# Attention kernel with a head mix: 64x64 mixing, the turn of E by R in two row halves, and k one step earlier

## The chip, the cores and the metric

One NeuronCore of a Trainium2 chip runs the whole program. The metric is the device time of one execution in microseconds (us). The engines are TensorE (PE: matrix products; its weight loads are shown as PEld), VectorE (DVE), ScalarE (ACT), GpSimd (POOL) and SyncE (SP, which issues most DMAs). Everything is fp32. An fp32 product shows in the trace as two passes, each a weight load and a MATMUL: "x8" for four products is eight passes.

## The reference

The input x has 8 batches of 512 tokens with 256 features. The program is half a step of an FFN block, an attention block and half a step of the FFN block again; only the attention is touched (and its constants, which are built during the first FFN). Cut to what matters:

```
q, k, v = x@Wq, x@Wk, x@Wv             # 16 heads of 64; 4 memory keys/values are put in front
dots = (l2norm(q) . l2norm(k)) * 10     # [16 heads, 512 queries, up to 516 keys]
dots = einsum('hg,bgij->bhij', W_pre_th, dots)    # every head becomes a mix of the 16 heads
dots = mask(causal); keep the 64 largest of a row, the others are masked
attn = softmax(dots)
attn = einsum('hg,bgij->bhij', W_post_th, attn)   # mixed over the heads again
out  = (attn @ v) * head_scale * sigmoid(x@Wg + bg) @ Wo
```

## The kernel before

**Units of work.** A tile t is 128 tokens (32 tiles; t % 4 is its place in its batch, here called tile 0 to 3 of the batch). A half u is 64 tokens. A group n is 8 queries with all 16 heads, 128 rows in all; a tile has 16 groups, and its step g (0, 2, ... 14) handles the pair of groups g and g+1. The width of a group is its number of live keys: 12 for the first of a batch, 8 more for each next one, 516 for the last. So tile 0 has widths 12 to 132, tile 1 140 to 260, tile 2 268 to 388, tile 3 396 to 516.

**The way of a group.** (1) PE computes raw scores of a half in four quarters (`score`, L1025): 64x64 products, four of them next to each other in the array, into bankD; ACT copies them to SC (L1241). (2) SP brings a group's scores with one DMA into 128 rows, raw[n] (L951). (3) PE mixes the heads (`mix`, L1036): one 128x128 stationary matrix `mixpre`, which is zero between different queries, and raw[n] streaming, into bankB; ACT writes it to S (L1252, L1255). (4) POOL adds the diagonal mask (L1387) and sets a first threshold (L1396), DVE takes row maxima and finds the 64th largest (`row_max`, `select_pair`), ACT counts signs (L1262, L1270) and takes the exponential (L1278), DVE zeroes what is below the limit and sums (L1559), then takes the reciprocal (L1563). (5) POOL scales the second mixing matrix by it: R = mixpost * rinv, 128x128 (L1403). (6) PE turns and mixes at once (`turn`, L1052): for each block of 128 keys E's block (128x128) is stationary and R (128x128) streams, which gives keys x (head, query) in bankC; a group of tile 0 has one block, of tile 3 four. ACT copies it into PT (`out_PT`, L1288). (7) PE multiplies PT with V (`attend`, L1078), and later projects (L1098).

**The order.** All engines run one loop over pairs n0, each with its own list of what comes in a step. PE in step n0 does mix(n0), a piece of projection, transpose or score, mix(n0+1), then turn(n0-6) and turn(n0-5), then another piece, then a piece of attend. The pieces: step 0 has xT (the transpose of the next tile's input) and the q projection of the next tile; step 2 score 0 and 1 of the second half (with the v projection in tile 1); step 4 score 2 (with v in tile 0) and the k projection of the next tile; step 6 score 3 and the gates; step 8 the transposes qT and kT (L1007); steps 10 to 14 the scores of the next tile's first half. ACT's list runs parallel to it: evict(n0), the first piece, evict(n0+1), sign counts, out_PT of the two groups turned, the second piece, exp of the pair before. `project_qk` on ACT (L1184, L1187) squares and copies q or k, and waits before k's square for `ssq_done` of q, since both use the tile qksq.

DVE sums the squares (`squares`, L1474, L1475): of q of tile t+1 at its own step 14 of tile t-1, of k at its step 2 of tile t; both in its list behind select_pair of that step. DVE is about two steps behind PE and ACT: select_pair of step 14 runs while PE is in steps 0 and 2 of the next tile. POOL makes the norms (`norm`, L1377 and L1381) at its steps 4 and 6; qT and kT on PE wait for them. The banks of bankD are used in one fixed order, the list `uses`; each use waits until ACT has read the banks' last one.

## Time and profile before

| | |
|---|---|
| median of 3 runs | 2355.67 us (2355.18 to 2355.76) |
| the profiled execution | 2356.68 us, its span 2354.8 us, mean granted clock of TensorE 0.952 of full speed |
| busy share of the span | PE 89%, PEld 58%, DVE 77%, ACT 68%, POOL 35% |
| L1052, turn: PE busy | 351.7 us for 2560 passes |
| L1036, mix: PE busy | 353.9 us for 1024 passes |
| L1025, scores: PE busy | 191.0 us for 2304 passes |

The attention takes the middle of the span, from about 207 to 2140 us; the two FFN blocks stand before and after it. Its eight batches repeat one pattern, slice by slice. Busy times of PE are modelled from the starts of pipelined instructions, so a duration of one MATMUL is longer than the step from one to the next; the starts are what tells the rate.

### The profile page before, as it was taken

What the parts mean: (1) busy time and instruction counts of PE and PEld (TensorE: products, weight loads), DVE (VectorE), ACT (ScalarE), POOL (GpSimd) and SP (SyncE); (2) the same over time, 40 slices, a digit from 0 to 9 for tenths busy, and PEclk for the clock granted to TensorE, in tenths of its full rate; (3) what the DMA queues carried; (4) which work ended last, traced back from release to release, by engine and by line L of the source; (5) the groups of instructions that cost most, each with busy time, mean ns of one, the idle gap of its engine ahead of it and who ended that gap; (6) DMA issues with size and microseconds to landing.
All of it is one profiled execution on the core that took longest, in us unless ns stands there. A gap on an engine that the chain in (4) does not pass through costs nothing. (4 is left out here: it accounts for less than half of the span.)

```text
span 2354.8 us, 55179 instructions
## 1 busy us (share of the span) xinstructions
PE 2106.7 (89%) x16059; PEld 1369.2 (58%) x16060; DVE 1803.1 (77%) x7282; ACT 1608.3 (68%) x4676; POOL 822.6 (35%) x2274
## 2 busy tenths in 40 slices
PE   7995699999999999999999999999899889985997
PEld 3433456666666666666666666666666666663433
DVE  6565389968996899689958995899589959993446
ACT  4442578857885788688858885888688758861543
POOL 3001444444444443444344434443443344311000
PEclk9996799999999999999999999999999999987998
DMA  5002012111211121012101211121012101212002
GB/s 175 0 0 85 22 40 61 43 25 43 61 43 26 43 61 43 25 43 61 43 25 43 61 43 25 43 61 43 26 43 61 43 23 41 58 38 87 1 0 72
DMA packets 113217, 104.69 MB, mean 44 GB/s; under 512 B 34449, under 2 KB 110865, under 8 KB 112913
## 3 DMA queue, kind: packets, MB, share of 16 engines
q1 hardware_dynamic: 108000, 96.65, 16.1%
q10 hardware_dynamic: 4912, 4.46, 0.6%
q8 instruction: 134, 2.20, 0.4%
q14 instruction: 171, 1.39, 0.2%
HBM read 19.14 MB, written 12.71 MB: 14 GB/s over the span
## 5 line engine op out<-in xcount | busy, mean ns | idle before, releaser
L1052 PE MATMUL bankC<-R,E 128*128 128x128 f32 x2560 | 351.7, 287 | 40.0 <-POOL R L1403 39.9
L1052 PEld LDWEIGHTS bankC<-R,E 128*128 128x128 f32 x2560 | 338.5, 202 | 76.3 <-POOL R L1403 43.9
L1036 PE MATMUL bankB<-raw,mixpre 128*128 128x76 f32 (+37 forms) x1024 | 353.9, 433 | 19.7 <-DMA raw<-SC 19.4
L1252 ACT ACTIVATE S<-bankB,aim_first 128x68 f32<-128x68 f32 (+56 forms) x456 | 232.3, 513 | 163.7 <-PE bankB L1036 163.3
L1499 DVE TENSOR_SCALAR_CACHE_REDUCE S<-S,minus_thr 128x68 f32<-128x68 f32 (+56 forms) x456 | 218.5, 515 | 139.4 <-POOL minus_thr L1396 137.8
L1387 POOL TENSOR_TENSOR S<-S,diagmask 128x8 f32<-128x8 f32 x512 | 106.8, 213 | 522.5 <-ACT S L1252 484.5
L1403 POOL TENSOR_SCALAR R<-mixpost,rinv 128x128 f32<-128x128 f32 x512 | 184.3, 372 | 284.9 <-DVE rinv L1563 284.5
L1559 DVE SCALAR_TENSOR_TENSOR E<-S,limit,E 128x68 f32<-128x68 f32 (+56 forms) x456 | 221.3, 521 | 35.1 <-ACT E L1278 5.2
L1278 ACT ACTIVATE E<-S,nmax 128x12 f32<-128x12 f32 (+56 forms) x512 | 240.0, 528 | 0.7 <-POOL nmax L1417 0.7
L1078 PEld LDWEIGHTS bankM<-PT,V 128*64 128x64 f32 x5120 | 179.0, 138 | 101.4 <-issue 90.9
L1036 PEld LDWEIGHTS bankB<-raw,mixpre 128*128 128x128 f32 x1024 | 159.7, 192 | 120.4 <-issue 82.5
L1078 PE MATMUL bankM<-PT,V 128*64 128x64 f32 x5120 | 227.8, 230 | 0.9 <-DVE gate L1483 0.9
L1025 PE MATMUL bankD<-KT,QT 64*64 64x132 f32 (+8 forms) x2304 | 191.0, 406 | 33.1 <-ACT SC L1241 23.6
L1288 ACT COPY PT<-bankC 128x512 f32<-128x512 f32 (+3 forms) x512 | 194.2, 432 | 36.4 <-PE bankC L1052 31.4
L1270 ACT ACTIVATE junk_side<-S 128x68 bf16<-128x68 f32 (+56 forms) x456 | 200.0, 448 | 15.8 <-DVE S L1499 15.8
L1377 POOL TENSOR_TENSOR rn<-ssq,neghalf 128x16 f32<-128x16 f32 x64 | 186.5, 2914 | 39.3 <-DVE ssq L1475 39.1
L1534 DVE MATCH_REPLACE8 near<-top,near 128x68 f32<-128x68 f32 (+56 forms) x456 | 200.1, 446 | 0.0
L1262 ACT ACTIVATE junk_first<-S 128x60 bf16<-128x60 f32 (+56 forms) x456 | 197.8, 447 | 0.3
L1529 DVE MAX8 top<-near 128x8 f32<-128x68 f32 (+56 forms) x456 | 187.7, 452 | 0.3
L1538 DVE MAX8 top<-near 128x8 f32<-128x68 f32 (+56 forms) x456 | 186.9, 450 | 0.3
L1241 ACT COPY SC<-bankD 128x136 f32<-128x136 f32 (+7 forms) x256 | 167.2, 653 | 21.6 <-PE bankD L1025 20.8
L1524 DVE TENSOR_SCALAR near<-S,flip 128x68 int32<-128x68 int32 (+56 forms) x456 | 150.1, 370 | 0.0
(177 smaller groups left out, 3935.4 us busy)
## 6 DMA issues: line engine op xcount, KB each, us to landing
X_first<-in_L_attn_x_dram ACTq DMA_DIRECT2D x8, 512.0 KB, 10.4
x<-X_first SPq DMA_DIRECT2D x8, 512.0 KB, 2.9
xt<-x SPq DMA_DIRECT2D x32, 128.0 KB, 2.4
x<-xt SPq DMA_DIRECT2D x32, 128.0 KB, 2.5
X_last<-x SPq DMA_DIRECT2D x8, 512.0 KB, 6.6
out_dram<-X_last SPq DMA_DIRECT2D x8, 512.0 KB, 2.8
raw<-SC SPq DMA_DIRECT2D x8, 258.0 KB, 2.9
raw<-SC SPq DMA_DIRECT2D x8, 254.0 KB, 3.1
```

The costliest lines, as they stand in the source:

```text
L1025: last = nc.tensor.matmul(bankD[cols, r, i * s[3]:(i + 1) * s[3]], QT[rows, pair, HALF * hh:HALF * hh + HALF], KT[rows, pair, first:first ...
L1036: last = nc.tensor.matmul(bankB[n % 2][:, 0:wide(n)], W.mixpre[:, :], raw[n % RAWS][:, 0:wide(n)], start=True, stop=True)
L1052: last = nc.tensor.matmul(bankC[n % 2][:, jb * P:(jb + 1) * P], E[n % EBUFS][:, jb * P:(jb + 1) * P], R[n % RBUFS][:, :], start=True, stop ...
L1078: last = nc.tensor.matmul(bankM[64 * lo:64 * lo + 64, pair * HALF:(pair + 1) * HALF], V[:, slot(t - blocks + 1 + jb), h * DH:(h + 1) * DH] ...
L1252: nc.scalar.activation(S[n % SBUFS][:, 0:wide(n)], src, ACT.Identity, bias=W.aim_first[:, group(n)]).then_inc(S_out, 1)
L1262: nc.scalar.activation(junk_first[n % 2][:, 0:w], S[n % SBUFS][:, 0:w], ACT.Sign, scale=-1.0, accum_out=below[:, col(n)]).then_inc(below_d ...
L1270: nc.scalar.activation(junk_side[n % 2][:, 0:w], S[n % SBUFS][:, 0:w], ACT.Sign, accum_out=signs[:, col(n)]).then_inc(signs_done, 1)
L1278: nc.scalar.activation(E[n % EBUFS][:, 0:w], S[n % SBUFS][:, 0:w], ACT.Exp, bias=nmax[:, col(n)]) \
L1288: last = nc.scalar.copy(PT[u % 2][:, 0:blocks, :, at:at + IG], bankC[n % 2][:, 0:blocks * P].rearrange("p (j h i) -> p j h i", h=H, i=IG))
L1499: nc.vector.tensor_scalar(row, row, minus_thr[:, col(n)], None, ALU.add, ALU.max, accum_out=rmax[:, col(n)]).then_inc(max_done, 1)
L1534: at[n] = step(nc.vector.match_replace(out=row, in_to_replace=top[n % 2][:, 8 * r - 8:8 * r], in_values=row, imm_value=-FMAX))
L1559: at[n] = step(nc.vector.scalar_tensor_tensor(out=E[n % EBUFS][:, 0:w], in0=S[n % SBUFS][:, 0:w], scalar=least, in1=E[n % EBUFS][:, 0:w], ...
```

## The change

It has four parts, and small ones that follow from them.

1. **Head mix in 64x64.** The queries of a pair of groups are dealt out so that the first 64 rows of raw hold four queries and the last 64 four others; mixpre becomes 64 columns wide. `mix_pair` computes both groups with four 64x64 products, one in each quadrant of the array (rows r, columns cols), into the two banks bankB, and comes at the start of a step; ACT evicts both groups right behind it. It takes the place of mix(n0) and mix(n0+1). The raw DMA of the even group brings 8 more columns.
2. **Scores in 64x32.** To put queries in that order, a score product is cut in two with 32 stationary columns each: 16 products of 64x64 for a half become 32 of 64x32, eight places in the array for each quarter. The copy to QT is cut in two (L1219).
3. **The turn in two row halves.** R becomes 128x64. `turn_pair` has for each group and block two products, one for each half of the rows: stationary 64x128 of E, streaming 64x64 of R, each half into its own bank of bankC; one increment for the pair. ACT's out_PT copies bank by bank, both groups in one instruction, with the same number of elements. The last group of a tile, whose memory-tail product needs all columns, gets a full matrix Rlast from POOL.
4. **k sooner.** The k projection moves from step 4 to step 2 on PE and ACT, score 1 from step 2 to 4, score 2 behind the turn of step 4, v of tile 1 from step 2 to 4; POOL's norms move from steps 4 and 6 to 2 and 4, and k's squares on DVE from step 2 to 0.

The core of the diff (the building of constants, which grows by 22 small DVE instructions, and the lists on ACT, which mirror PE's, are cut):

```diff
@@ -1018,46 +1031,58 @@
                     def emit():
                         first, quarters = (512, range(4)) if s[2] == "last" else (0, (q,))
                         for i, quarter in enumerate(quarters):
-                            for side_ in range(2):
+                            for c, side_ in ((0, 0), (0, 1), (1, 0), (1, 1)):
                                 for r in range(2):
-                                    rows, cols = slice(64 * r, 64 * r + 64), slice(64 * side_, 64 * side_ + 64)
-                                    pair = 4 * side_ + quarter
-                                    last = nc.tensor.matmul(bankD[cols, r, i * s[3]:(i + 1) * s[3]],
-                                                            QT[rows, pair, HALF * hh:HALF * hh + HALF],
-                                                            KT[rows, pair, first:first + s[3]],
+                                    rows, at = slice(64 * r, 64 * r + 64), 64 * c + 32 * side_
+                                    pair, lo = 4 * side_ + quarter, HALF * hh + 32 * c
+                                    last = nc.tensor.matmul(bankD[at:at + 32, r, i * s[3]:(i + 1) * s[3]],
+                                                            QT[rows, pair, lo:lo + 32], KT[rows, pair, first:first + s[3]],
                                                             start=True, stop=True, skip_group_check=True)
                         return last
                     pe_use(pe, s, emit)
 
-            def mix(n):
-                pe.wait_ge(raw_in[n % RAWS], 16 * (n // RAWS + 1))
-                if n >= 2:
-                    pe.wait_ge(S_out, n - 1)
-                last = nc.tensor.matmul(bankB[n % 2][:, 0:wide(n)], W.mixpre[:, :], raw[n % RAWS][:, 0:wide(n)],
-                                        start=True, stop=True)
-                if is_wide(n):
-                    if n // GPT >= 2:
-                        pe.wait_ge(x_added, n // GPT - 1)
-                    last = nc.tensor.matmul(bankT[:, P:P + MEM], W.mixpre[:, :], raw[n % RAWS][:, 512:J],
-                                            start=True, stop=True)
-                last.then_inc(mixed, 1)
-
-            def turn(n):
-                t, g = divmod(n, GPT)
-                pe.wait_ge(R_ready, n + 1)
-                pe.wait_ge(E_zero, EBUFS * (n // GPB) + min(n % GPB, EBUFS - 1) + 1)
-                if n >= 2:
-                    pe.wait_ge(PT_out, n - 1)
-                for jb in range(t % TPB + 1):
-                    last = nc.tensor.matmul(bankC[n % 2][:, jb * P:(jb + 1) * P], E[n % EBUFS][:, jb * P:(jb + 1) * P],
-                                            R[n % RBUFS][:, :], start=True, stop=True)
-                if g == GPT - 1:
+            def mix_pair(n0):
+                for n in (n0, n0 + 1):
+                    pe.wait_ge(raw_in[n % RAWS], 16 * (n // RAWS + 1))
+                if n0:
+                    pe.wait_ge(S_out, n0)
+                parts = [(r, cols, slice(HALF * r, HALF * r + HALF), raw[(n0 + (r + cols) % 2) % RAWS])
+                         for cols in range(2) for r in range(2)]
+                if is_wide(n0 + 1):
+                    if n0 // GPT >= 2:
+                        pe.wait_ge(x_added, n0 // GPT - 1)
+                    for r, cols, rows, src in parts:
+                        if r:
+                            nc.tensor.matmul(bankT[HALF * cols:HALF * cols + HALF, P:P + MEM], W.mixpre[rows, :],
+                                             src[rows, 512:J], start=True, stop=True, skip_group_check=True)
+                for r, cols, rows, src in parts:
+                    w = wide(n0 + r)
+                    last = nc.tensor.matmul(bankB[r][HALF * cols:HALF * cols + HALF, 0:w], W.mixpre[rows, :],
+                                            src[rows, 0:w], start=True, stop=True, skip_group_check=True)
+                last.then_inc(mixed, 2)
+
+            def turn_pair(n0):
+                t, g = divmod(n0, GPT)
+                last_n = n0 + 1
+                pe.wait_ge(R_ready, last_n + 1)
+                pe.wait_ge(E_zero, EBUFS * (last_n // GPB) + min(last_n % GPB, EBUFS - 1) + 1)
+                if n0:
+                    pe.wait_ge(PT_out, n0)
+                for r in range(2):
+                    n = n0 + r
+                    for jb in range(t % TPB + 1):
+                        for c in range(2):
+                            rows, at = slice(HALF * c, HALF * c + HALF), 256 * r + HALF * jb
+                            last = nc.tensor.matmul(bankC[:, c, at:at + HALF], E[n % EBUFS][rows, jb * P:(jb + 1) * P],
+                                                    R[n % RBUFS][rows, :], start=True, stop=True, skip_group_check=True)
+                if g == GPT - 2:
                     tail = (t % TPB + 1) * P
+                    pe.wait_ge(last_ready, t + 1)
                     if t >= 2:
                         pe.wait_ge(x_added, t - 1)
-                    last = nc.tensor.matmul(bankT[0:MEM, 0:P], E[n % EBUFS][:, tail:tail + MEM], R[n % RBUFS][:, :],
+                    last = nc.tensor.matmul(bankT[0:MEM, 0:P], E[last_n % EBUFS][:, tail:tail + MEM], Rlast[:, :],
                                             start=True, stop=True)
-                last.then_inc(turned, 1)
+                last.then_inc(turned, 2)
 
             def attend(u, pairs):
                 t, hh = divmod(u, 2)
@@ -1110,13 +1135,13 @@
                 t, g = divmod(n0, GPT)
                 live, ahead = n0 < NG, t + 1 < NT
                 if live:
-                    mix(n0)
+                    mix_pair(n0)
                     if g == 0 and ahead:
                         xT(t + 1)
                     if g == 2:
                         score(2 * t + 1, 0)
                     if g == 4:
-                        score(2 * t + 1, 2)
+                        score(2 * t + 1, 1)
                     if early_values(t, g):
                         tokens(t, "v", Wv, slice(0, P))
                     if g == 6:
@@ -1127,18 +1152,15 @@
                         score(2 * t + 2, 1)
                     if g == 14 and ahead:
                         score(2 * t + 2, 3)
-                    mix(n0 + 1)
                 if n0 >= LAG:
-                    turn(n0 - LAG)
-                if n0 >= LAG:
-                    turn(n0 + 1 - LAG)
+                    turn_pair(n0 - LAG)
                 if live:
                     if g == 0 and ahead:
                         tokens(t + 1, "q", Wq)
-                    if g == 2:
-                        score(2 * t + 1, 1)
-                    if g == 4 and ahead:
+                    if g == 2 and ahead:
                         tokens(t + 1, "k", Wk)
+                    if g == 4:
+                        score(2 * t + 1, 2)
                     if g == 8 and ahead:
                         turn_qk(t + 1, 1, "kT")
                     if g == 10 and ahead:
@@ -1278,20 +1305,23 @@
                 nc.scalar.activation(E[n % EBUFS][:, 0:w], S[n % SBUFS][:, 0:w], ACT.Exp, bias=nmax[:, col(n)]) \
                     .then_inc(exp_done, 1)
 
-            def out_PT(n):
-                t, g = divmod(n, GPT)
-                u = n // IG
-                act.wait_ge(turned, n + 1)
-                if n % IG == 0 and u >= 2:
+            def out_PT(n0):
+                t, g = divmod(n0, GPT)
+                u = n0 // IG
+                act.wait_ge(turned, n0 + 2)
+                if n0 % IG == 0 and u >= 2:
                     act.wait_ge(attended, u - 1)
-                blocks, at = t % TPB + 1, n % IG * IG
-                last = nc.scalar.copy(PT[u % 2][:, 0:blocks, :, at:at + IG],
-                                      bankC[n % 2][:, 0:blocks * P].rearrange("p (j h i) -> p j h i", h=H, i=IG))
-                if g == GPT - 1:
+                blocks, at = t % TPB + 1, n0 % IG * IG
+                dst = PT[u % 2][:, 0:blocks, :, at:at + 2 * IG].rearrange("p j h (z i) -> p z (j h) i", z=4)
+                for c in range(2):
+                    src = bankC[:, c, :].rearrange("p (r x) -> p r x", r=2)[:, :, 0:blocks * HALF]
+                    last = nc.scalar.copy(dst[:, 1:3, :, :] if c else dst[:, 0:4:3, :, :],
+                                          src.rearrange("p r (x i) -> p r x i", i=QUARTER))
+                if g == GPT - 2:
                     if t:
                         act.wait_ge(attended, 2 * t)
                     last = nc.scalar.copy(PTtail[:, :, :], bankT[0:MEM, 0:P].rearrange("p (h i) -> p h i", i=IG))
-                last.then_inc(PT_out, 1)
+                last.then_inc(PT_out, 2)
 
             xT(0)
             project_qk(0, 0, "q")
@@ -1400,6 +1429,11 @@
                 pool.wait_ge(E_ready, n + 1)
                 if n >= RBUFS:
                     pool.wait_ge(turned, n - RBUFS + 1)
+                if n % GPT == GPT - 1:
+                    if n >= GPT:
+                        pool.wait_ge(turned, n - GPT + 1)
+                    nc.gpsimd.tensor_scalar(Rlast[:, :], W.mixlast[:, :], rinv[:, col(n)], 1.0, ALU.mult,
+                                            ALU.mult).then_inc(last_ready, 1)
                 nc.gpsimd.tensor_scalar(R[n % RBUFS][:, :], W.mixpost[:, :], rinv[:, col(n)], 1.0, ALU.mult,
                                         ALU.mult).then_inc(R_ready, 1)
 
@@ -1432,9 +1466,8 @@
                 if live and ahead:
                     if g == 2:
                         copy_halo(t + 1)
+                        norm(t + 1, 0)
                     if g == 4:
-                        norm(t + 1, 0)
-                    if g == 6:
                         norm(t + 1, 1)
                 if live and g == 8 and t + 2 < NT:
                     ln_rstd(t + 2)
@@ -1600,7 +1633,7 @@
                     squares(t + 2, 0)
                 if g == 6 and t >= 2:
                     residual(t - 2)
-                if g == 2 and t and t + 1 < NT:
+                if g == 0 and t and t + 1 < NT:
                     squares(t + 1, 1)
                 if (n0 + 2) % GPB == 0:
                     mark_batch(n0 // GPB)
```

The other hunks give the widths and names above (`QUARTER = 4`, `V1_AT = 4`, mixpre, mixpost, mixlast, a mask for either group of a pair, R, Rlast, one two-bank bankC, `last_ready`), the same order in `uses` and on ACT, and the copy to QT in two.

## Rows read from the trace of the kernel before

**Rows 1.** The page: busy time and share of each engine.

```profile
PE 2106.7 (89%) x16059; PEld 1369.2 (58%) x16060; DVE 1803.1 (77%) x7282; ACT 1608.3 (68%) x4676; POOL 822.6 (35%) x2274
```

**Rows 2.** Windows, a tile each (tiles 1, 2, 3, next 0), columns in the first row.

```profile
core 0: us, PE busy (x) PEld busy (x) DVE busy (x) ACT busy (x) POOL busy (x), PEclk, DMA share, GB/s
...
1467.00:1525.00 58.00, 53.78 (x380) 35.86 (x382) 46.80 (x228) 44.19 (x154) 24.39 (x64) 0.97 0.17 44
1525.00:1585.00 60.00, 57.77 (x472) 37.90 (x474) 56.00 (x226) 52.45 (x149) 25.10 (x64) 1.00 0.25 60
1585.00:1653.00 68.00, 61.85 (x620) 45.09 (x615) 65.47 (x224) 54.11 (x139) 24.55 (x58) 0.95 0.16 37
1653.00:1700.00 47.00, 41.68 (x413) 30.14 (x414) 26.83 (x168) 28.81 (x112) 25.28 (x63) 1.00 0.12 31
```

**Rows 3.** Waits in these windows: PE in tiles 1, 2, 3, 0; DVE in tile 2.

```profile
engine line waited for: us in total, times, longest us
PE bankD L1007 <- POOL qk L1381: 2.2, 1, 2.2
...
PE bankD L1007 <- POOL qk L1381: 1.6, 1, 1.6
...
PE bankC L1052 <- POOL R L1403: 4.2, 1, 4.2
...
PE bankB L1036 <- DMA raw<-SC: 2.4, 2, 1.8
...
PE bankD L1007 <- POOL qk L1381: 1.1, 1, 1.1
...
DVE S L1499 <- POOL minus_thr L1396: 1.5, 2, 1.2
```

**Rows 4.** Timeline of PE, steps 2 and 4 of a tile 0.

```profile
start us, us, engine line op out<-in xcount [idle before <-releaser]
...
1647.11 0.46 PE L1025 MATMUL bankD<-KT,QT 64*64 64x132 f32 x8
1647.50 0.41 PE L1036 MATMUL bankB<-raw,mixpre 128*128 128x36 f32 x2
1647.74 2.03 PE L1052 MATMUL bankC<-R,E 128*128 128x128 f32 x16
1649.70 0.46 PE L1025 MATMUL bankD<-KT,QT 64*64 64x132 f32 x8
1650.09 1.62 PE L1078 MATMUL bankM<-PT,V 128*64 128x64 f32 x48
...
1658.95 3.70 PE L984 MATMUL bankD<-Wk,xnT 128*128 128x512 f32 x8
1662.58 1.15 PE L1078 MATMUL bankM<-PT,V 128*64 128x64 f32 x32
```

**Rows 5.** Timeline of PE's weight loads: mix (128x128) here.

```profile
1647.49 0.30 PEld L1036 LDWEIGHTS bankB<-raw,mixpre 128*128 128x128 f32 x2 [0.18 <-issue]
```

**Rows 6.** The same in the last FFN: two row halves of 64x128.

```profile
2200.07 0.30 PEld L371 LDWEIGHTS ffn_pair_out<-ffn_h,cn_w4r 64*128 64x128 f32 x4 [0.76 <-issue]
```

**Rows 7.** Timeline of DVE, end of a batch's last select_pair.

```profile
1653.34 0.17 DVE L1563 RECIPROCAL rinv<-rsum 128x2 f32<-128x2 f32 x1
...
1654.70 0.57 DVE L1475 TENSOR_SCALAR ssq<-ssq 128x16 f32<-128x16 f32 x1
```

**Rows 8.** Timeline of ACT, reading the first half of k.

```profile
1661.05 0.60 ACT L1184 ACTIVATE qksq<-bankD 128x512 f32<-128x512 f32 x1 [1.26 <-PE bankD L984]
1661.55 0.58 ACT L1187 COPY qk<-bankD 128x512 f32<-128x512 f32 x1
```

**Rows 9.** Timeline of PE, step 0 of a tile 0, clock at half.

```profile
1637.46 3.78 PE L1052 MATMUL bankC<-R,E 128*128 128x128 f32 x16 [4.22 <-POOL R L1403]
```

**Rows 10.** Timeline of POOL: the norm of q.

```profile
1659.25 2.92 POOL L1377 TENSOR_TENSOR rn<-ssq,neghalf 128x16 f32<-128x16 f32 x1
1662.25 1.90 POOL L1381 TENSOR_TENSOR qk<-qk,rn 128x1024 f32<-128x1024 f32 x1
```

**Rows 11.** Timeline of PE, start of a tile 1.

```profile
1691.14 0.51 PE L1036 MATMUL bankB<-raw,mixpre 128*128 128x140 f32 x2 [1.76 <-DMA raw<-SC]
...
1692.50 0.52 PE L1036 MATMUL bankB<-raw,mixpre 128*128 128x148 f32 x2 [0.63 <-DMA raw<-SC]
```

**Rows 12.** Windows: the stretch of the first FFN that builds the constants.

```profile
110.00:140.00 30.00, 30.00 (x77) 11.28 (x76) 26.41 (x86) 13.93 (x20) 1.09 (x2) 1.00 0.00 1
```

84 lines of the change are left out of this document (51 added, 33 removed).

## The prediction

> **What bounds the kernel now.** The page first: PE is busy 89% of the span, DVE 77% [rows 1]. A mean over stages says little here, so the windows of one batch come next, a tile each [rows 2]. In tiles 2 and 3 DVE is busy 56.0 of 60 us and 65.5 of 68. In tile 1 it is busy 46.8 of 58, in tile 0 26.8 of 47: there PE decides. There PE is busy 53.8 of 58 and 41.7 of 47 us, and stands still for things that a faster DVE would not bring: 2.2 us for qk in tile 1, 1.1 us for qk and 2.4 us for a raw DMA in tile 0 are the largest [rows 3]. Tile 3 has 4.2 us in which PE waits for R, that is for DVE [rows 3]. So a microsecond of PE counts in full in tiles 0 and 1; in tile 2 at most the 1.5 us that DVE waits there [rows 3]; in tile 3 nothing.
>
> **The turn, part by part.** Sixteen 128x128 passes start at 1647.74 and the next product at 1649.70 [rows 4]: 1.96 us, of which the way into another tile shape is 0.17 (below), so 0.112 us a pass. What sets it? Two passes of mix with only 36 streaming columns are 0.24 us long (1647.50 to 1647.74) [rows 4], as are their loads [rows 5]: a load of 128 stationary columns takes 0.11 us however little streams. The new turn streams half as many columns, but each load still has 128. Can the two row halves load at once? The last FFN has two 64x128 products side by side: their four loads take 0.30 us together, as long as the two loads of one 128x128 product [rows 5, 6]. So yes, and a pair of half passes costs what one whole pass did, 0.112 us. I put the saving in the turn at nothing; both ends stay open (half the passes' time if loads overlapped further, double if they came one after the other). The Trainium skill ("TensorEngine Tiling (Array Packing)", Theoretical Speedup) gives up to 2x where the contraction is 64 or less; the sum with that rule is a rival below.
>
> **The mix.** Before, a pair of groups costs four passes, each the larger of 0.11 us and its columns at 0.84 ns (512 columns take 0.43: eight passes and one change of shape in 3.63 us [rows 4]). After, four quadrants run together, as the scores do now: eight passes of 132 columns in 0.39 us [rows 4] are two times 0.11 and a change. So a pair costs two passes, with loads of 64 columns. Tile 0: 32 passes of 0.11 = 3.5 us become 16 of about 0.08 = 1.3 us, saves 2.2. Tile 1 (mean width 200): 32 of 0.17 become 16 of 0.17, saves 2.7. Tile 2 saves 4.4.
>
> **The changes of shape.** What takes part of this back: where PE goes from one tile shape to another, the next weights can't be loaded ahead. Score to mix: 0.39 us for two steps of 0.11 leaves 0.17; score to attend, 1649.70 to 1650.09, the same 0.17 [rows 4]; turn to score 1.96 less 16 x 0.112, again 0.17. I take 0.16. Before, all mixes, turns and projections are 128x128. Counting step by step through PE's list, a tile has 25 changes. After, mix is 64x64, score 64x32, turn 64x128, attend 128x64, the rest 128x128: 37. Twelve more cost 1.9 us a tile. Net: tile 0 +0.3 us, tile 1 +0.8, tile 2 +2.5. No row shows a change from 64x64 to 64x32 (about six of the 37); between nothing and 0.16 I take 0.16, as all rows show it. The Trainium skill (the same page, Key Properties) has a change of mode drain the engine, which would hold for these six too.
>
> **The scores.** Each quarter has eight 64x32 products in place of four of 64x64, with the same streaming columns. If all eight run together the time is the same; the loads are shorter, the issues twice as many. No row shows more than four. Cost: nothing to one more time the streaming; I take nothing, from the four that do run together.
>
> **k sooner.** qT and kT stop waiting for POOL: its norm takes 2.9 + 1.9 us [rows 10] and both norms now come a step (6 to 8 us) sooner, more than any of these waits. That gives 2.2 us in tile 1, 1.1 in tile 0, and 1.6 in tile 2 that DVE mostly hides [rows 3].
> But it makes a new wait at each border from tile 3 to the next batch's tile 0. ACT may square k only after DVE has summed q's squares, and DVE does this behind the last select_pair of the batch, ready at 1655.27 [rows 7]. PE's turn of step 2 ends at 1649.70 [rows 4]; k's first half (four passes, 1.7 us) is then ready at 1651.4, and ACT stands 3.9 us, with exp and evict of the next step queued behind. It reads k in 2.2 us (both halves, [rows 8]), until 1657.5. PE goes on with the second half, attend (1.6) and mix_pair, until about 1654.9, then score 1 needs both banks: 2.6 us idle. At the three other borders DVE is little behind and the wait is under 1 us, beside other work. Idle PE has a second price: after the 4.2 us wait for R, the same 16 passes took 3.78 us instead of 1.96 [rows 9, 4], PE at half its clock. One such stretch costs 1.8 to 2.4 us; I count a quarter, 0.6.
>
> **Pairs in place of singles.** At the start of tile 1 PE waits for raw twice, 1.76 and 0.63 us [rows 11]. mix_pair waits for both, and xT and its copy, which lay between, now come behind it, as does the copy behind two evictions: 0.9 us more in tile 1, 0.2 in tile 0, and 0.2 for v in tile 1, since ACT copies the score behind two evictions too. POOL's q norm now waits for DVE and holds back a threshold in tile 2: 0.4 us.
>
> **At nothing:** out_PT (same elements; ACT has 7.5 us of slack in tile 2 [rows 2]); POOL's R half as wide and one Rlast a tile (POOL is busy 25 of 60); 8 more columns in half the DMAs; 22 more DVE instructions in the first FFN, where PE is busy all 30 us [rows 12] and DVE isn't: some 3 us there, in DVE's 3.6 us of idle time, and on PE's path only if more.
>
> **The sum,** for one batch: tile 0 +0.3 +1.1 -2.6 -0.6 -0.2 = -2.0 us; tile 1 +0.8 +2.2 -0.9 -0.2 = +1.9; tile 2 +1.5 -0.4 = +1.1; tile 3 none. Saved 1.0 us a batch. Seven batches 7, and the first, with no border before it, 1.0 + 3.2: 11.2 us. The profiled execution took 2356.7 us around a span of 2354.8; less 11.2 is 2345.5. It lies 1.0 above the median of the runs, so the forecast is 2344.5 us for the median. About 0.2% (4.7 us) is what a measurement of this kernel can tell from no change.
>
> **Rivals.**
> *The border wait costs nothing.* If k's first half comes later than I think, or PE has other work, the 3.2 us of wait and half clock vanish in seven batches: 22 more, 2322 us. For it: PE is behind DVE at other borders. Against: the times of rows 4 and 7.
> *The turn does get faster.* By the skill's rule above it would take half. In tile 0 three pairs still have four blocks and five have one: 17 block pairs of four passes, 7.6 us; in tile 1, three of one and five of two, 5.8. Half of both is 6.7 us a batch, 54 in all: about 2290. Against: loads of 128 columns set the pace already [rows 5].
> *Slower: the border wait with the clock.* Place: step 4 of tile 0. If the idle 2.6 us, with less work in the narrow mixes, takes PE to half clock each time, a stretch costs the full 2.4 us and not 0.6; and if a change of shape costs 0.2 us and not 0.16 (0.5 us a tile, 1.0 for tiles 0 and 1), a batch is 1.0 - 1.8 - 1.0 = 1.8 us longer, 2356 + 14 = 2369 us. It decides once both prices together pass 1.0 us a batch.
> *The scores' eight products don't run together.* Their streaming comes twice: 16 passes of 0.14 in tile 0 = 2.2 us, in tile 1 of 0.24 = 3.9, in tile 2 hidden by what mix gives back. Then a batch is 5.1 us longer, 41 in all: 2397 us.
> *The row halves load one after the other.* 2560 passes more at 0.112 us, 287 us less what tile 3 hides: above 2550. Rows 6 speaks clearly against.
> *The parts cancel:* within 5 us of 2355.7, of which no single row decides.
>
> **Chances.** The forecast 0.38, no border wait 0.20, the faster turn 0.04, slower by border and clock 0.19, cancelled 0.09, scores one after the other 0.07, loads one after the other 0.03. The forecast's own spread puts 0.05 of it within 0.2%, and 0.02 of the slower case too. Faster: 0.33 + 0.20 + 0.04 = 0.57; same: 0.09 + 0.05 + 0.02 = 0.16; slower: 0.27. The range holds the forecast, no border wait and the slower case with their spread: 2316 to 2380; the faster turn and the two large losses, 0.14, stay outside, and some spread.
>
> **What would show it.** Turn: L1052's passes double to about 5120, in pairs of starts a few ns apart, one pair each 0.11 us; 0.06 would be the rule, 0.22 the serial loads. Mix: 2048 passes, four together, PE busy on it down from 353.9 to about 200 us. Scores: x16 for a quarter in 0.4 us at 132 columns. The waits for qk (L1007) are gone; in their place, once a batch, k's square on ACT waits for ssq, and PE's score 1 waits for ACT's copy of k by some 2.6 us. Tiles 2 and 3 keep their length to 1.5 us. The forecast is wrong if tile 0 gets shorter, or tile 3 changes by over 1 us: then DVE's chain, which I leave alone, has moved.

## The result and the profile after

The changed kernel takes 2361.86 us (median of eight runs, 2357.89 to 2363.74), the kernel before beside it 2355.19: a ratio of 1.0025, 95% interval 1.0016 to 1.0034. The forecast was 2344.5, so the direction was wrong, by little but beyond the interval; the value lies in the forecast's range of 2316 to 2380. The profiled execution took 2357.89 us (span 2356.1, granted clock 0.918 of full speed, before 0.952), 4 us under its own median.

The page of the changed kernel: busy time of the engines, then three groups of PE (line, operation, out<-in, shapes, count | busy us, mean ns | idle before).

```profile
PE 2068.9 (88%) x21963; PEld 1291.0 (55%) x21964; DVE 1808.0 (77%) x7304; ACT 1594.9 (68%) x4740; POOL 800.3 (34%) x2306
...
L1076 PE MATMUL bankC<-R,E 64*128 64x64 f32 x5120 | 377.8, 297 | 46.2 <-POOL R L1437 46.2
...
L1038 PE MATMUL bankD<-KT,QT 64*32 64x68 f32 (+8 forms) x4608 | 195.6, 400 | 77.6 <-ACT SC L1268 44.3
...
L1060 PE MATMUL bankB<-raw,mixpre 64*64 64x512 f32 (+61 forms) x2048 | 180.7, 419 | 40.9 <-DMA raw<-SC 37.5
```

PE's busy time on mix halves, 353.9 to 180.7 us, the scores cost 4.6 more, the turn 26 more. PE is busy 38 us less than in [rows 1], and the span does not get shorter: PE stands still longer. The windows of one batch (tiles 1, 2, 3, next 0, columns as in [rows 2]):

```profile
1467.00:1521.00 54.00, 50.07 (x524) 30.31 (x525) 46.70 (x228) 44.15 (x158) 23.99 (x66) 1.00 0.19 48
1521.00:1579.00 58.00, 55.35 (x646) 34.15 (x644) 55.52 (x226) 52.48 (x149) 24.24 (x63) 1.00 0.27 62
1579.00:1651.00 72.00, 60.64 (x826) 44.60 (x826) 65.67 (x227) 51.75 (x134) 23.27 (x59) 0.83 0.16 36
1651.00:1702.00 51.00, 45.35 (x616) 30.88 (x616) 26.96 (x164) 28.94 (x119) 24.55 (x64) 0.90 0.12 30
```

Tiles 1 and 2 are shorter, tiles 3 and 0 longer, and in these two the clock is at 0.83 and 0.90. What PE waits for over the whole span now:

```profile
engine line waited for: us in total, times, longest us
PE bankC L1076 <- POOL R L1437: 46.2, 24, 5.5
...
PE bankD L1038 <- ACT SC L1268: 44.3, 59, 1.8
PE bankB L1060 <- DMA raw<-SC: 37.5, 19, 3.2
PE bankD L1038 <- ACT qk L1209: 29.8, 32, 2.2
PE bankD L997 <- ACT SC L1268: 22.7, 47, 1.8
...
PE bankD L1020 <- POOL qk L1410: 6.7, 2, 3.7
```

The waits for qk from POOL [rows 3], 52.8 us in all in the kernel before, are gone within the tiles; the two that are left (6.7 us) lie ahead of the first tile. In their place PE waits for ACT (97 us in the three lines, 44 before) and for raw (37.5, 19.4 before). The timeline of PE in tile 3, steps 4 and 6 (a line's last bracket is PE's idle time before it, and what ended it):

```profile
1580.34 0.96 PE L1060 MATMUL bankB<-raw,mixpre 64*64 64x428 f32 x8
1582.95 1.09 PE L1038 MATMUL bankD<-KT,QT 64*32 64x512 f32 x16 [1.65 <-ACT qk L1209]
...
1589.79 1.09 PE L1038 MATMUL bankD<-KT,QT 64*32 64x512 f32 x16 [1.02 <-ACT SC L1268]
1592.70 0.80 PE L1038 MATMUL bankD<-KT,QT 64*32 64x4 f32 x64 [1.82 <-ACT SC L1268]
1593.43 3.68 PE L1076 MATMUL bankC<-R,E 64*128 64x64 f32 x32
1597.03 6.23 PE L1009 MATMUL bankD<-xnT,Wg 128*128 128x128 f32 x32
```

After three stretches of idle time the same 32 half passes take 3.68 us that take 2.00 elsewhere in this tile, and the gates 6.23 in place of the 3.84 that they take in tile 0. The granted clock over the turn is 0.50 (1.2 GHz), over the gates 0.59. ACT gets the gates late, POOL the scores, and DVE, which sets the pace of this tile, stands still:

```profile
1609.66 0.69 DVE L1532 TENSOR_SCALAR_CACHE_REDUCE S<-S,minus_thr 128x460 f32<-128x460 f32 x1 [3.10 <-POOL minus_thr L1425]
```

It goes by the clock in the other batches too: in batches 2 to 7 turn and gates of this step take 9.9, 9.7, 8.4, 9.9, 9.8 and 7.3 us together, and their tile 3 is 72.0, 71.8, 70.5, 72.0, 71.9 and 69.6 us long. DVE stands still 3.2 us in such a tile, 0.1 in the kernel before.

The border wait of the forecast is there too, at step 4 of tile 0. ACT's wait for DVE's sum of squares is 3.2 to 4.0 us at all seven borders. One of them, then PE's timeline behind it:

```profile
ACT qksq L1206 <- DVE ssq L1508: 3.3, 1, 3.3
```

```profile
1655.44 0.46 PE L1038 MATMUL bankD<-KT,QT 64*32 64x132 f32 x16 [1.17 <-ACT qk L1209]
1656.52 5.37 PE L997 MATMUL bankD<-Wv,xnT 128*128 128x512 f32 x8 [0.62 <-ACT SC L1268]
```

In tile 1, PE's waits of 1.76 and 0.63 us for raw [rows 11] have become one of 2.81, and the q projection behind it takes 5.10 us (3.60 there before), at half clock for its first part (0.72 over the whole):

```profile
1692.44 0.77 PE L1060 MATMUL bankB<-raw,mixpre 64*64 64x140 f32 x8 [2.81 <-DMA raw<-SC]
...
1694.81 5.10 PE L997 MATMUL bankD<-Wq,xnT 128*128 128x512 f32 x8
```

### The profile page after: what moved, and what is told of

It is laid out like the page before. It is cut to its first block and busy times, and to the rows that moved or that the text cites. A ratio compares the mean times of both kernels' runs of the same rounds, so it can differ in the third digit from the quotient of the medians.

```text
span 2356.1 us, 66666 instructions
## 1 busy us (share of the span) xinstructions
PE 2068.9 (88%) x21963; PEld 1291.0 (55%) x21964; DVE 1808.0 (77%) x7304; ACT 1594.9 (68%) x4740; POOL 800.3 (34%) x2306
## 5 line engine op out<-in xcount | busy, mean ns | idle before, releaser
L1076 PEld LDWEIGHTS bankC<-R,E 64*128 64x128 f32 x5120 | 340.8, 206 | 156.5 <-issue 89.0
L1076 PE MATMUL bankC<-R,E 64*128 64x64 f32 x5120 | 377.8, 297 | 46.2 <-POOL R L1437 46.2
L1279 ACT ACTIVATE S<-bankB,aim_first 128x68 f32<-128x68 f32 (+56 forms) x456 | 207.4, 511 | 115.0 <-PE bankB L1060 115.0
L1592 DVE SCALAR_TENSOR_TENSOR E<-S,limit,E 128x68 f32<-128x68 f32 (+56 forms) x456 | 234.2, 549 | 51.1 <-ACT E L1305 24.1
L1437 POOL TENSOR_SCALAR R<-mixpost,rinv 128x64 f32<-128x64 f32 x512 | 157.5, 320 | 339.5 <-DVE rinv L1596 338.8
L1038 PE MATMUL bankD<-KT,QT 64*32 64x68 f32 (+8 forms) x4608 | 195.6, 400 | 77.6 <-ACT SC L1268 44.3
L1103 PE MATMUL bankM<-PT,V 128*64 128x64 f32 x5120 | 233.3, 233 | 0.9 <-DVE gate L1516 0.9
L1060 PE MATMUL bankB<-raw,mixpre 64*64 64x512 f32 (+61 forms) x2048 | 180.7, 419 | 40.9 <-DMA raw<-SC 37.5
L1206 ACT ACTIVATE qksq<-bankD 128x512 f32<-128x512 f32 x128 | 76.9, 601 | 126.9 <-PE bankD L997 75.9
L997 PE MATMUL bankD<-Wq,xnT 128*128 128x512 f32 x256 | 146.7, 726 | 5.9 <-ACT xnT L1195 5.5
```

The source lines that it names most:

```text
L1038: last = nc.tensor.matmul(bankD[at:at + 32, r, i * s[3]:(i + 1) * s[3]], QT[rows, pair, lo:lo + 32], KT[rows, pair, first:first + s[3]], s ...
L1076: last = nc.tensor.matmul(bankC[:, c, at:at + HALF], E[n % EBUFS][rows, jb * P:(jb + 1) * P], R[n % RBUFS][rows, :], start=True, stop=True ...
L1103: last = nc.tensor.matmul(bankM[64 * lo:64 * lo + 64, pair * HALF:(pair + 1) * HALF], V[:, slot(t - blocks + 1 + jb), h * DH:(h + 1) * DH] ...
L1279: nc.scalar.activation(S[n % SBUFS][:, 0:wide(n)], src, ACT.Identity, bias=W.aim_first[:, group(n)]).then_inc(S_out, 1)
L1592: at[n] = step(nc.vector.scalar_tensor_tensor(out=E[n % EBUFS][:, 0:w], in0=S[n % SBUFS][:, 0:w], scalar=least, in1=E[n % EBUFS][:, 0:w], ...
```

## The experiments

All were timed in five rounds beside the kernel before. The table has the median, the ratio with its interval, and, from the profiled run, where the stretches begin and end by the reciprocals (L1563 before): the time to the end of the first batch, the mean length of tiles 0 to 3 in the next six batches, the last batch, and what follows it. Executions of one kernel scatter, and not by the same amount: the five of e2 lie between 2312.7 and 2324.4 us, the six of e3 between 2336.2 and 2349.1. The profiled one of e3 is its fastest, 8.8 us under its median; those of after and e9 lie 4.0 below and 3.5 above theirs. So the last few us of a difference between two rows should not be read.

```
                     median  ratio (95%)             first | tile 0     1     2     3 |  last | rest
before              2355.19                          484.2 |  47.09 57.87 60.34 68.41 | 231.2 | 237.2
after               2361.86  1.0025 (1.0016-1.0034)  478.0 |  50.62 53.83 58.66 71.29 | 226.5 | 245.2
e1_old_k            2409.12  1.0221 (1.0207-1.0234)  492.7 |  49.32 58.91 61.48 69.10 | 233.6 | 245.2
e2_only_k           2323.71  0.9846 (0.9828-0.9865)  475.2 |  49.53 53.59 58.49 68.83 | 226.4 | 237.8
e10_..not_tile0     2308.14  0.9801 (0.9787-0.9815)  468.8 |  47.85 53.65 58.51 68.84 | 224.1 | 238.0
e3_k_tiles_12       2344.97  0.9955 (0.9941-0.9969)  482.9 |  49.54 53.82 58.63 68.92 | 227.1 | 238.9
e7_k_and_scores     2327.36  0.9885 (0.9870-0.9899)  474.5 |  49.57 53.98 58.56 68.68 | 225.3 | 237.1
e13_pair_order      2339.87  0.9920 (0.9903-0.9937)  472.1 |  50.66 53.90 58.99 69.86 | 226.6 | 239.0
e9_whole_turn       2349.85  0.9980 (0.9972-0.9989)  473.6 |  52.20 53.84 58.62 70.33 | 228.5 | 239.4
e8_k_and_turn       2374.00  1.0081 (1.0061-1.0101)  479.7 |  51.16 54.54 59.82 71.13 | 230.2 | 246.5
e4_act_order        2346.95  0.9962 (0.9949-0.9975)  480.7 |  49.85 53.54 58.63 70.28 | 226.0 | 245.2
e6_filler_tile3     2339.00  0.9925 (0.9911-0.9938)  476.8 |  49.99 53.82 58.62 69.56 | 229.0 | 239.5
e11_turn_fill_R     2375.87  1.0079 (1.0062-1.0097)  481.7 |  51.50 54.55 59.83 70.08 | 229.6 | 246.2
e14_turn_fill_3     2374.90  1.0079 (1.0065-1.0092)  479.9 |  51.78 54.56 59.82 70.86 | 228.2 | 246.6
e12_k_fill          2300.76  0.9760 (0.9747-0.9773)  470.3 |  47.46 53.23 58.53 68.30 | 223.0 | 238.6
e15_k_fill_short    2283.80  0.9694 (0.9680-0.9707)  470.4 |  45.08 53.20 58.56 68.33 | 221.3 | 237.3
e16_all_mended      2346.39  0.9959 (0.9945-0.9972)  476.5 |  51.11 53.53 58.64 68.30 | 229.7 | 248.3
e17_mended_fill     2321.48  0.9864 (0.9844-0.9883)  480.9 |  47.17 53.40 58.69 69.35 | 225.5 | 240.6
```

**The two halves of the change: e1 and e2.** e1 is the changed kernel with the order of pieces of before, e2 the kernel before with the new order alone.

```diff
# e1, and the reverse on the kernel before for e2 (cut: scores 1 and 2, v of tile 1,
# POOL's norms and DVE's squares move with k)
-                    if g == 2 and ahead:
+                    if g == 4 and ahead:
                         tokens(t + 1, "k", Wk)
```

> New mix, scores and turn, but the order of pieces of before (k in step 4, score 1 in step 2, the norms and squares with them). Theory A (the new order costs: at the batch's border and in tile 3 PE stands still for ACT, and falls to half its clock): tile 0 falls back from 50.6 to about 48, tile 3 from 71.8 to about 68.5, tiles 1 and 2 lose 2.2 and 1 us to the qk wait again; a batch 3 us shorter than with the whole change, 2335 to 2345 us. Theory B (the new tile shapes cost, through changes of shape and a lower clock, and k sooner gains): no better than the whole change, 2360 to 2375 us, tile 3 stays near 71.

> The kernel before with the new order of pieces alone (k in step 2, and what goes with it); mix, scores and turn as before. Theory A: tile 0 at 50 or more and tile 3 above 70, tiles 1 and 2 shorter by about 2 and 1 us: 2362 to 2380 us, slower than the whole change, since the mix saves nothing. Theory B: faster than before by the waits for qk, about 3 us a batch: 2330 to 2345 us.

k sooner gains 31 us by itself and 47 on the new shapes; the new shapes cost 54 us with the old order and 38 with the new one. So the small loss is the sum of two large terms of opposite sign. e1 lies far outside both of its ranges: tile 3 does fall to 69.1 (theory A), but tiles 1 and 2 lose 5.1 and 2.8 us, and the total is 34 us above the higher of them. e2 is faster than theory B's range, by 6 us. In e2 tiles 1 and 2 fall to 53.6 and 58.5 us and stay there in every later kernel with this order but for e8 and its kin: what is gained on PE beyond this point is not seen in them. Tile 1 gains more than the 2.2 us of its qk wait, since the clock fell behind that wait: in the kernel before it is 0.70 and 0.74 in the two stretches of 3 us from 1491 to 1497 us, some 1.7 us of work lost, and 1.00 in all of tile 1 in e2.

**Where k sooner pays: e10 and e3.** In e10, e2's order holds but for tile 0 of the later batches. e3 is the whole change with k sooner in tiles 1 and 2 only.

```diff
+        def sooner(t):
+            return t % TPB in (1, 2, 3) or t == 0     # e10; in e3: t % TPB in (1, 2)
```

> The kernel with k sooner alone, but tile 0 of all batches except the first has the order of before (k in step 4). If the wait of ACT for DVE's sum of q's squares at the border is what made tile 0 go from 46.6 to 49.7 us there, tile 0 is 47 again and the total 2324 less 7 x 3 = 2303 (2300 to 2312) us. If tile 0's new order costs and gives the same, 2318 to 2328 us.

> The whole change, but k sooner in tiles 1 and 2 of a batch alone; tiles 0 and 3 have the order of before. Theory A: tiles 1 and 2 as with the whole change (53.9 and 58.6), tiles 0 and 3 near 47.5 and 68.5: 2362 less 7 x 6 = about 2320 (2312 to 2335), the best of all. Theory B: tiles 0 and 3 stay long, 2350 to 2365 us.

e10 is 15.6 us faster than e2. By the reciprocals the border wait with its clock costs 1.7 us a batch in tile 0, 12 us over seven borders; the first batch, where both kernels run the same list up to its last steps, ends 6.4 us sooner in e10 all the same, which the edit does not explain. The forecast had 2.6 and 0.6. e3 is 17 us faster than the whole change, and its tile 3 is back at 68.9: in tile 3 the new shapes and the pairs without k sooner cost 0.5 us, k sooner without them 0.4 (e2, 68.8), both together 2.9. But e3's total lies between its two ranges: its tile 0 stays at 49.5, where theory A had 47.5.

**The shapes one at a time: e7, e13, e9, e8.** e7 is e2 with the 64x32 scores. e13 is e7 with both mixes at the start of a step behind one wait for both, still as whole passes. e9 is the whole change with whole passes in the turn. e8 is e2 with the turn in row halves.

```diff
# e7 (cut: the places in QT and bankD)
-                            for side_ in range(2):
+                            for c, side_ in ((0, 0), (0, 1), (1, 0), (1, 1)):
# e13 (cut: the waits; ACT evicts both groups right behind)
                     mix(n0)
+                    mix(n0 + 1)
...
-                    mix(n0 + 1)
# e9, R 128 columns wide, an out_PT for each group
-                    turn_pair(n0 - LAG)
+                    turn(n0 - LAG)
+                    turn(n0 + 1 - LAG)
# e8: the reverse of e9, on e2, R 64 columns wide
```

> The kernel with k sooner alone (2324 us), and the scores in 64x32 products, eight next to each other, at the places in bankD where they were; mix and turn as before. If the eight don't all run together, or the smaller tiles lower the clock, 2340 to 2370 us. If the cost lies in the turn or in the pairs, within 4 us of 2324.

> k sooner and the scores in 64x32 (2327.4), mix still in whole passes of 128x128, but both mixes of a pair at the start of the step, behind a wait for both raw tiles and both evictions, and ACT evicts both first. The whole change but for the turn (2349.9) has this order and the 64x64 mix. Theory A: the order in pairs is what costs, tile 0 gets 2.5 to 3 us longer and tile 3 about 2, and the run is at 2345 to 2360, since the mix itself is not shorter. Theory B: the changes of tile shape in and out of the 64x64 mix cost, the order nothing: 2325 to 2332.

> The whole change, but R 128 wide and the turn in whole passes, one group after the other, with an out_PT for each, as before; the mix in 64x64 pairs, the scores in 64x32 and k sooner stay. If the turn carries the loss, 2325 to 2340 us. If the mix in pairs or the scores do, 2355 to 2365 us, as the whole change.

> The kernel with k sooner alone (2324 us), and the turn in two row halves, a pair of groups at once, with R 64 wide; scores and both single mixes as before, in shape and place (mixpre's columns are in another order). If the turn in halves carries the loss (16 changes of shape more a tile, PE waits for both groups' R, ACT for both turns), 2340 to 2360 us. If it is free, within 4 us of 2324. Faster than 2315 if halves cost less than whole passes after all.

The ladder is e2 2323.7, e7 2327.4, e13 2339.9, e9 2349.9, after 2361.9: the scores 3.6, the order in pairs 12.5, the 64x64 mix 10.0 more, the turn in halves 12.0 more. The scores' 3.6 is within the scatter (the profiled spans of e2 and e7 are 2322.0 and 2321.6). The turn's 12.0 isn't in the batches: with it the four tiles are together 0.6 us shorter than in e9, and what is longer is the first batch, 4.4, and the rest behind the last, 5.8. Alone, on e2, the turn in halves costs 50. Of the expectations e7's came true (within 4 us of 2324); e8 is 14 us above its range, e9 and e13 lie between their two.

The mix, half as long on PE, makes the kernel slower. From e13 to e9 it changes together with what its order of rows needs: ACT copies QT in two parts, its first eviction waits for both groups, and a tile has 30 changes of shape in place of 25. No run separates these. PE's idle time goes from 15.9 to 25.8 us a batch, in the 17 us ahead of the gates of tile 3 from 1.7 to about 5, and a batch is 1.6 us longer. How a wait comes about is seen beside tile 3 of e2 (PE's timeline, steps 4 and 6):

```profile
1559.28 1.09 PE L1025 MATMUL bankD<-KT,QT 64*64 64x512 f32 x8
1560.30 1.00 PE L1036 MATMUL bankB<-raw,mixpre 128*128 128x436 f32 x2
1561.13 1.50 PE L1052 MATMUL bankC<-R,E 128*128 128x128 f32 x12
...
1566.12 1.09 PE L1025 MATMUL bankD<-KT,QT 64*64 64x512 f32 x8 [0.36 <-ACT SC L1241]
1568.51 0.65 PE L1025 MATMUL bankD<-KT,QT 64*64 64x4 f32 x32 [1.30 <-ACT SC L1241]
```

There the second mix (1.00 us) lies between the pieces that wait for ACT, and PE stands idle 1.7 us; in the changed kernel both mixes lie in front and take 0.96, and PE stands idle 4.5 us in the same place. The saved work became a wait, and behind the wait the turn takes 3.61 us from start to next start in five of six batches of the changed kernel (in e2 1.78 in four and 2.6 in two).

The turn's price is another. Step 2 of tile 0, PE's timeline of e2 and of e8, where nothing waits:

```profile
1619.04 0.41 PE L1036 MATMUL bankB<-raw,mixpre 128*128 128x36 f32 x2
1619.28 2.03 PE L1052 MATMUL bankC<-R,E 128*128 128x128 f32 x16
1621.15 3.60 PE L984 MATMUL bankD<-Wk,xnT 128*128 128x512 f32 x8
1624.68 1.50 PE L1078 MATMUL bankM<-PT,V 128*64 128x64 f32 x44
```

```profile
1660.59 0.41 PE L1049 MATMUL bankB<-raw,mixpre 128*128 128x36 f32 x2
1660.93 2.00 PE L1070 MATMUL bankC<-R,E 64*128 64x64 f32 x32
1662.86 3.70 PE L997 MATMUL bankD<-Wk,xnT 128*128 128x512 f32 x8
1666.49 0.69 PE L1097 MATMUL bankM<-PT,V 128*64 128x64 f32 x16
```

From mix to attend it is 5.64 us with whole passes and 5.90 with halves: 0.26 for the two changes of shape around this turn, 0.13 each, and the passes themselves are no faster (2.03 and 2.00). Behind other turns the next piece had another shape before, too. Counted in the traces, a tile has 25 changes in e2 and 38 in e8 (not 16 more, as expected): 52 more a batch, 6.8 us at 0.13 each; the batches got 6.2 us longer. e8 also lets PE wait for both groups' R, and ACT for both turns, but that is not it: PE's idle time is 11.6 us a batch in e8 and 15.5 in e2.

**Tile 3: e4 and e6.** Both are the whole change. In e4, ACT evicts the second group behind the first piece, as before. In e6, PE has two filler products of 512 columns ahead of mix_pair in steps 4 and 6 of tile 3.

```diff
# e4
                     evict(n0)
-                    evict(n0 + 1)
...
+                if live:
+                    evict(n0 + 1)
                 for n in ranked_in(n0):
# e6
+                if n0 % GPB in (3 * GPT + 4, 3 * GPT + 6):
+                    for _ in range(2):
+                        nc.tensor.matmul(bankB[0][:, :], W.ident[:, :], ..., start=True, stop=True)
                 parts = [(r, cols, ...
```

> The whole change, but ACT evicts the second group of a pair behind the first piece again, not right behind the first group. If PE's waits in tile 3 for ACT's copy of the scores come from the two evictions ahead of it, tile 3 is 1 to 2 us shorter and the total 2348 to 2358 us. If ACT is simply full there, or the shapes are the cause, within 3 us of the whole change, 2359 to 2365.

> The whole change, with two filler products of 512 columns ahead of mix_pair at steps 4 and 6 of every tile 3 (into the bank of B that mix_pair writes next). In the changed kernel PE stands idle there three times (1.7, 1.0 and 1.8 us), the granted clock falls to half, and the turn takes 3.7 us and not 1.9, the gates 6.2 and not 3.6. If the idle PE's clock is what makes tile 3 longer (71.8 us against 68.3), tile 3 gets about 3 us shorter and the run 20 us: 2335 to 2350. If the wait itself is the cause (ACT with more to do in these steps), the filler changes nothing or costs its own 1.7 us a step: 2360 to 2375.

The filler adds 3.8 us of useless work to each tile 3 (1.91 a stretch) and the kernel gets 22.9 us faster, faster than the kernel before. PE's timeline in e6, the stretch of the one above:

```profile
1574.98 1.98 PE L1051 MATMUL bankB<-Wo,ident 128*128 128x512 f32 x4
1576.89 0.99 PE L1064 MATMUL bankB<-raw,mixpre 64*64 64x444 f32 x8
1577.81 1.09 PE L1038 MATMUL bankD<-KT,QT 64*32 64x512 f32 x16
1580.07 0.71 PE L1038 MATMUL bankD<-KT,QT 64*32 64x4 f32 x64 [1.17 <-ACT SC L1272]
1580.71 2.00 PE L1080 MATMUL bankC<-R,E 64*128 64x64 f32 x32
1582.65 5.46 PE L1009 MATMUL bankD<-xnT,Wg 128*128 128x128 f32 x32
```

The turn is back at 2.00 us; the clock still falls behind it, in the gates (5.46). Tile 3 is 1.7 us shorter, tile 0 0.6, and the rest after the last batch 5.7. The turn is at 1.93 to 1.98 us in all six batches, where the whole change had 3.61 in five: the cause in tile 3 is the clock. e16, below, has the clock at full in the gates as well, and there tile 3 is back at 68.3.

e4 is 14.9 us faster too, just beyond its range, with tile 3 1.0 us shorter. It is not less idle time: in the same stretch PE stands still 4.6 us and the turn takes 3.61. The gates are shorter (4.9 to 5.2 us), and ACT evicts the second group later; no run separates the two.

**The clock behind the row halves: e11 and e14, e12 and e15.** At each batch border PE waits 4.2 us for R and then runs at half clock. e11 (on e8) and e12 (on e10) fill this wait with eight products of 512 columns; e12 also fills the wait for raw at the start of tile 1 with three. e14 is e11 with three in place of eight, e15 is e12 with four and two. In all of them PE's wait for R now comes behind the filler.

```diff
# e15, on e10
+                if n % GPB == GPB - LAG:
+                    for _ in range(4):
+                        nc.tensor.matmul(bankC[n % 2][:, :], W.ident[:, :], ..., start=True, stop=True)
                 pe.wait_ge(R_ready, n + 1)
```

> The kernel of before with k sooner and the turn in row halves (2374.0), plus eight filler products of 512 columns (3.4 us) in PE's 4.2 us wait for R at each batch border. There the turn in row halves took 3.7 us at half clock and the q projection behind it 5.7 us, still at half; with whole passes the same turn took 3.8 us and the q projection 3.2. Theory A: half of the 50 us that the row halves cost is clock, since the clock stays at half behind them. Then with the filler the turn takes 1.9 and the q projection 3.1: 4.3 us a batch, seven batches, about 2344 us. Theory B: the 50 us are the changes of tile shape alone (12 more a tile, each 0.1 us), and the clock at the border is hidden: 2365 to 2375.

> As e11 (k sooner, the turn in row halves, filler in PE's wait for R at each batch border), with three filler products in place of eight. In e11 the filler ran 8.8 us where PE had 2.8 us left to wait, so that what it gave back (the turn 1.9 in place of 3.7 us, the q projection 3.0 in place of 5.7) it also took. Theory A (clock): now the overshoot is gone and tile 0 gets 3 to 4 us shorter than in e8 (51.12): about 2350 us. Theory B (the 50 us are the changes of shape): 2365 to 2375, tile 0 at 50 or more. Tiles 1 to 3 keep e8's lengths under both.

> The best kernel so far (k sooner, but not in tile 0 of a later batch, 2308.1), plus eight filler products in the wait for R at each batch border and three in the wait for raw at the start of each tile 1. Theory A (the clock's price at the border is on PE's path): the turn goes from 3.8 to 2.0 us, the q projections behind both waits from 3.4 to 3.0: 2.0 to 2.6 us a batch, 2290 to 2295 us. Theory B (ACT's chain sets tile 0): 2305 to 2311. If the filler is longer than the waits it costs up to 1 us each: 2312 to 2320.

> As e12 (the best so far, 2300.8), with four filler products in place of eight in the wait for R, and two in place of three in the wait for raw. In e12 step 2 of tile 0 was 1.45 us longer than without filler (9.59 against 8.14), as the filler overshot. If that counts: 1.0 to 1.5 us a batch, 2291 to 2295 us. If DVE or ACT has hidden it: 2299 to 2302. If four do not hold the clock: 2303 to 2308.

e14's timeline of PE at a border:

```profile
1409.43 2.00 PE L1074 MATMUL bankC<-R,E 64*128 64x64 f32 x32
1411.37 3.70 PE L997 MATMUL bankD<-Wq,xnT 128*128 128x512 f32 x8
...
1427.81 0.46 PE L1038 MATMUL bankD<-KT,QT 64*64 64x132 f32 x8 [2.67 <-ACT qk L1208]
```

The clock is held: from turn to attend it is 5.6 us and not 9.8 as in e8. The time does not change, though, since PE then waits 2.67 us for ACT, which waits for DVE's squares at its fixed place. So the clock was hidden at this border. In e11 the mean granted clock of the batches is higher than in e2 (0.983 and 0.972) and a batch still takes 236.0 us against 230.4. Theory B holds: what e8 loses is the changes of shape, 6.2 us a batch, and 8.7 us behind the last batch, where the clock is at half. e11 is 1 us above theory B's range, e14 inside it.

On e10, where ACT doesn't wait for the squares, the same filler pays. Eight products were too long (they ran past the end of the wait, 7.4 us gained, between the ranges of theories A and B); four and two give 24.3 us, more than the 13 to 17 I had expected. Windows of e15 (tiles 1, 2, 3, next 0):

```profile
1416.00:1469.00 53.00, 50.49 (x366) 33.52 (x366) 46.67 (x228) 43.30 (x151) 24.38 (x63) 1.00 0.19 48
1469.00:1527.00 58.00, 57.34 (x455) 37.65 (x454) 55.52 (x226) 52.56 (x148) 25.33 (x64) 1.00 0.26 61
1527.00:1596.00 69.00, 64.77 (x649) 45.53 (x648) 66.31 (x229) 54.09 (x141) 24.87 (x58) 1.00 0.17 37
1596.00:1641.00 45.00, 42.13 (x419) 30.38 (x417) 26.12 (x165) 28.86 (x113) 25.10 (x63) 1.00 0.13 33
```

The clock is at full from 260 to 2040 us. e15 beats both kernels: 2283.8 us, 3.06% less than before (2.93 to 3.20).

**All mended: e16 and e17.** e16 is the whole change with e10's order, e4's eviction and e6's filler; e17 has the fillers in the two waits as well.

> The whole change with what each experiment mended: the old order in tile 0 of the later batches, ACT's second eviction behind the first piece, and the filler in tile 3. Against e10 (2308.1) it has the three new shapes and the pairs as well. Theory A (waits and clock are all that the shapes cost): within 5 us of e10. Theory B (the changes of tile shape cost on their own, some 0.15 us each, and are not hidden in tile 0): tile 0 stays 1.5 to 3 us longer than e10's 47.84, and the run is at 2320 to 2335.

> e16 (the whole change with the waits mended, 2346.4, tile 0 at 51.4 us) with the filler of e15 as well: four products in the wait for R at each batch border, three in the wait for raw at the start of tile 1. In e16 the turn behind the wait for R takes 3.7 us and the q projection behind it 4.8 to 5.8, and the q projection of tile 1 4.8 to 5.7, all at half clock. Theory A (clock): with it at full, 1.7 + 2.3 + 2.0 us a batch less, tile 0 at 45.5 to 47.5 and the run at 2300 to 2320; against e15 (2283.8) what is left is then the price of the three shapes themselves. Theory B (the wait for raw, longer since it is for two tiles at once, holds tile 0, and ACT's chain fills the rest): 2335 to 2347.

e16 was a miss for theory A, and 11 us worse than I had put B: tile 3 is at 68.30, as good as without the shapes (turn 1.93 us and gates 3.77 in all six batches), but tile 0 is at 51.11 against e10's 47.85, with q projections of 6.1 to 6.4 us at six of the seven borders, and the rest behind the last batch is the longest of all. e17 gives 24.9 us back (tile 0 at 47.17, as theory A of that run said; the time is 1.5 above its range). What is left against e15 is 38.7 us of span: 10.5 up to the end of the first batch, 2.1 in tile 0 and 1.0 in tile 3 of each batch, 4.2 in the last, 3.3 behind it. That is what the three shapes and the pairs cost without the border wait, with tile 3's filler and with the clock that is still lost: 0.97 in tile 0 and 0.92 in tile 3, where e15 has 1.00; the gates of tile 3 are at half clock in four of six batches. No run takes these apart.

## Why the prediction was wrong

**Tile 3 is the step that failed**: "in tile 3 nothing", "tile 3 none". DVE's 65.5 of 68 us were read as room for PE. But tile 3 has a place where ACT is behind, and there PE's own work had been the cover. The forecast worked out what mix would save in tiles 0 to 2 and never asked where the saved time would stand. It stood as idle time in front of ACT (4.5 us), behind which turn and gates ran at half clock, and reached DVE through POOL's threshold (3.1 us): 2.9 us a tile. It takes the shapes and pairs together with k sooner (e3 without the latter: 0.5 us); e6 and e16 show that the clock carries it. The forecast had said that it was wrong if tile 3 changed by over 1 us.

**The rest behind the last batch** was not costed: 237.2 to 245.2 us. Of these 8.0 us 5.8 lie ahead of the last attend, a stretch of 11.8 us at full clock that becomes 17.6 at a mean clock of 0.59. The last attends, PE's timeline of after and of e2:

```profile
2117.57 1.12 PE L1103 MATMUL bankM<-PT,V 128*64 128x64 f32 x16 [0.95 <-DVE gate L1516]
```

```profile
2089.27 0.69 PE L1078 MATMUL bankM<-PT,V 128*64 128x64 f32 x16 [0.94 <-DVE gate L1482]
```

The same work behind the same wait, at half clock in the changed kernel. It occurs in most kernels whose turn is in halves, but not in e6, hardly in e17, and not in the profiled (fastest) execution of e3, so row halves alone do not bring it about. Why the clock falls there in one kernel and not in another stays open.

**Term by term**, predicted and measured for one batch: tile 0, 2.0 longer, 3.5: by the reciprocals the start of tile 1 counts here, with its wait for two raw tiles of 2.81 us and q at half clock behind it; e13 and e9 show this order and the shorter mix as 1.1 and 1.5 us of tile 0, where I had a gain from mix. Tile 1, 1.9 shorter, 4.0: k sooner gives back the clock behind the qk wait too. Tile 2, 1.1 shorter, 1.7. Tile 3, none, 2.9 longer. Together 1.0 shorter against 0.7 longer: 10 us over six batches; the rest behind the last adds 8. Up to the end of the first batch it is 6.2 us shorter (predicted 4.2), in the last batch 4.7 (predicted 1.0). That makes the 12.5 us between the predicted span, 2343.6, and the measured one, 2356.1.

**What held.** The turn's rate: 32 half passes in 2.00 us, a pair every 0.112 us, one whole pass's time. The rival that the turn takes half the time is refuted. The Trainium skill ("TensorEngine Tiling (Array Packing)", Theoretical Speedup) gives up to 2x for a contraction of 64; the turn here gained nothing of it. The changes of shape: 25 and 37 a tile, as counted, and 0.26 us for two, 0.13 each, where I took 0.16. The Trainium skill (the same page, Key Properties) has a change of mode drain the engine; the rows agree in that each change costs time. But I set this price against mix's gain alone: e8 shows that the turn in halves has its own share and nothing to set against it. The scores: nothing beyond the scatter; their eight products do run together (x16 of 132 columns in 0.39 us, as the x8 before). The border wait: ACT 3.2 to 4.0 us for ssq (forecast 3.9), and PE idle behind it, 1.17 us where I had 2.6 (2.67 in e14, where the clock ahead of it is held). Its price is seen only without the shapes, 1.7 us a batch (e10); there ACT waits longer, 4.8 to 5.7 us. The rival "slower by border and clock" had the right kind of mechanism and the wrong place: the clock was lost in tile 3, and behind the wait for raw. Its sum, 2356 + 14, is 2370 and not 2369, and no row gives the 2.4 us for a stretch at half clock that both it and the 0.6 go by; rows 4 and 9 give 1.8. That the result lies in the range is luck. The forecast's terms, added up by cause, give k sooner 16 us of gain and the shapes and pairs 5 us of loss; measured are 31 (e2) and 38. Errors of 15 and 33 us partly cancel.

## What to carry to other kernels

Work taken from an engine is worth something only where that engine is not waiting a little later: look for the next wait on its list, and add the saved microseconds to it first. On TensorE such a saving can cost more than it brings, since the clock can be at half for the work behind the idle time, as in tile 3 here; useless products in a long wait, cut to fit inside it, are worth testing early (24 us here), and they pay only where what follows the wait is on the path (e14 gained nothing). And count changes of tile shape like instructions: splitting a product in halves whose loads set the pace gave nothing here and paid for the way in and the way out.
